# Prototype logits as extra columns of a values product, and FFN statistics and normalisation spread over the ratio attention and GpSimd

## The reference, cut to what matters

```python
x = x + _L0_xattn_ref(_layernorm(x), ctx, ctx, ...)   # distance attention
x = x + _L0_attn_ref(_layernorm(x), ...)              # ratio attention, causal
x = x + _L0_ffn_ref(_layernorm(x), ...)               # 4-bit weights, activations quantised
x = x + _L1_xattn_ref(_layernorm(x), ctx, ...)        # context attention
x = x + _L1_attn_ref(_layernorm(x), ...)              # segment attention
x = x + _L1_ffn_ref(_layernorm(x), ...)               # two of eight experts

# in _L0_ffn_ref: one scale for the whole tensor, from its largest magnitude
scale = jnp.maximum(jnp.max(jnp.abs(x)) / qmax, 1e-12)
x = jnp.clip(jnp.round(x / scale), -qmax - 1.0, qmax) * scale

# in _L1_attn_ref, x the normalised input (32 tokens a batch, 8 prototypes)
long_out = _mha(x, lt_w_in, lt_b_in, lt_w_out, lt_b_out, H)
seg = jnp.argmax(x @ protos.T, axis=-1)
same = seg[:, :, None] == seg[:, None, :]
short_out = _mha(x, st_w_in, st_b_in, st_w_out, st_b_out, H, mask=same)
short_out = jnp.where((tok_cnt == 1)[..., None], x, short_out)
combined = jnp.concatenate([long_out, short_out], axis=-1) @ fus_w.T + fus_b
```

## Time and profile before

| what | us |
|---|---|
| median of 3 runs | 754.5 (753.74 to 754.9) |
| the profiled execution | 752.91 |
| its span | 751.1 |
| TensorE busy | 662.8 (88% of the span), weight loads 500.4 |
| VectorE busy | 485.5 (65%) |
| ScalarE busy | 365.0 (49%) |
| GpSimd busy | 310.1 (41%) |
| distance attention | 0 to about 262 |
| ratio attention | about 262 to 334 |
| FFN, from its statistics to the down products | about 334 to 447 |
| context attention | about 447 to 500 |
| segment attention | about 500 to 613 |
| experts | about 613 to 751 |

### The profile page before, as it was taken

The page is one execution under the profiler, slowest core; times in us unless marked ns, Lnnn a source line. Parts: engine busy times, 40 slices in busy tenths (PEclk is TensorE's granted clock), DMA queues, the critical chain, the costliest instruction groups (busy, mean ns, idle before and its releaser), DMA issues.

```text
span 751.1 us, 16917 instructions
## 1 busy us (share of the span) xinstructions
PE 662.8 (88%) x6115; PEld 500.4 (67%) x6115; DVE 485.5 (65%) x1367; ACT 365.0 (49%) x992; POOL 310.1 (41%) x458
## 2 busy tenths in 40 slices
PE   4899999999999989985994799988999776999990
PEld 3677878787777778753443586667877673777760
DVE  2686777677768669885488873558888875333330
ACT  1454545545555479874395653436566431222320
POOL 1235455646453179850000031136556513556541
PEclk9999999999999999996997699999999986999995
DMA  8723222322220000019200434538001022243434
GB/s 265 245 62 79 64 78 65 78 65 75 68 72 14 1 3 4 3 44 332 103 0 1 156 125 177 217 125 367 2 3 65 3 99 53 47 69 58 68 40 70
DMA packets 31697, 65.08 MB, mean 87 GB/s; under 512 B 5792, under 2 KB 21792, under 8 KB 29312
## 3 DMA queue, kind: packets, MB, share of 16 engines
q1 hardware_dynamic: 26016, 55.73, 22.8%
q0 software_dynamic: 4688, 7.18, 6.0%
q10 hardware_dynamic: 912, 1.10, 0.5%
HBM read 57.67 MB, written 7.37 MB: 87 GB/s over the span
## 4 chain that ended last, share of the span: by engine, by line
PE 64%; DVE 21%; ACT 5%; issue 4%; DMA 2%; SPq 2%; POOL 1%; DVEq 0%; ACTq 0%; POOLq 0%
PE psum L2627 7%; PE psum L474 6%; PE psum L482 6%; PE psum L496 5%; PE psum L2637 4%; PE psum L521 4%; PE psum L507 4%; PE psum L1482 3%; PE psum L1459 3%; PE psum L837 2%; DVE ff_peak L1500 2%; PE psum L846 2%; PE psum L829 2%; PE psum L877 2%; DMA wn<-in_w_down 2%
## 5 line engine op out<-in xcount | busy, mean ns | idle before, releaser
L415 ACT ACTIVATE prob<-s_sb,negm 128x257 f32<-128x257 f32 x128 | 66.2, 517 | 94.5 <-DVE negm L640 94.5
L782 POOL TENSOR_SCALAR bias<-dist,cst 128x257 f32<-128x257 f32 x128 | 59.8, 486 | 99.5 <-DVE dist L627 89.6
L636 DVE CUSTOM_DVE_ANT_0 s_sb<-psum,bias 128x257 f32<-128x257 f32 x128 | 49.4, 423 | 51.7 <-PE psum L496 48.4
L474 PE MATMUL psum<-ctxT,shared 128*128 128x257 f32 x256 | 62.6, 388 | 2.7 <-DMA msk<-in_mask 2.7
L482 PE MATMUL psum<-shared,ctxT 128*128 128x256 f32 x256 | 60.4, 379 | 0.0
L2627 PE MATMUL psum<-ex_w,shared 128*128 x184 | 58.3, 460 | 0.6 <-ACT shared L2520 0.6
L1721 POOL TENSOR_TENSOR wn<-wn,cst 128x1 f32<-128x1 f32 x8 | 4.7, 589 | 120.4 <-DVE wn L1848 120.4
L474 PEld LDWEIGHTS psum<-ctxT,shared 128*128 128x128 f32 x256 | 47.2, 195 | 9.0 <-issue 3.4
L482 PEld LDWEIGHTS psum<-shared,ctxT 128*128 128x128 f32 x256 | 48.4, 189 | 6.8
L496 PE MATMUL psum<-kT,qbd 64*128 64x257 f32 x256 | 48.4, 429 | 3.0 <-DVE mx L636 2.9
L2627 PEld LDWEIGHTS psum<-ex_w,shared 128*128 128x128 f32 x184 | 33.1, 190 | 15.4 <-issue 0.8
(11 more groups left out here) (359 smaller groups left out, 1655.9 us busy)
## 6 DMA issues: line engine op xcount, KB each, us to landing
ctxT<-in_ctx_T SPq DMA_DIRECT2D x32, 257.0 KB
ex_w<-in_w SPq DMA_DIRECT2D x1, 5632.0 KB, 17.5
kpos<-in_kpos SPq DMA_DIRECT2D x32, 128.5 KB
msk<-in_mask SPq DMA_DIRECT2D x32, 128.5 KB
near_turned<-in_ctx_T_tiles SPq DMA_DIRECT2D x4, 1028.0 KB
ff_used_up<-in_ctx_T_tiles SPq DMA_DIRECT2D x4, 1028.0 KB
near_rows<-in_ctx_tiles SPq DMA_DIRECT2D x4, 1024.0 KB, 8.0
ff_used_up<-in_ctx_tiles SPq DMA_DIRECT2D x4, 1024.0 KB, 7.3
```

The costliest lines, as they stand in the source:

```text
L415: nc.scalar.activation(prob[n % 2][:, g, :], s_sb[n % 2][:, g, :], ACT.Exp, bias=negm[:, b, g:g + 1], accum_out=esum[t % 2][:, b, g:g + 1]) \
L474: ins = nc.tensor.matmul(kv[m][:, 0:SK], w["xa_k"][:, k, P * m:P * m + P], ctxT[n % BT][:, k, :], start=(k == 0), stop=(k == KT - 1))
L636: nc.vector.tensor_tensor_reduce(s_sb[n % 2][:, g, :], sc[g % 2][:, 0:SK], bias[n % 2][:, g, :], 1.0, float("-inf"), ALU.add, ALU.max, mx[ ...
L782: nc.gpsimd.tensor_scalar(bias[n % 2][:, g, :], dist[n % 2][:], c.slope[:, g:g + 1], 1.0, ALU.mult, ALU.mult).then_inc(bias_ready, 1)
```

## The change

It does the following:

- A class `FeedNorm` holds statistics, variances and roots of the FFN's input. It is allocated ahead of the ratio attention. VectorE's `feed_stats(n)` (statistics, aggregate, variance of one tile) is called in ratio slots 3 to 7 for tiles 0 to 4, between the subtraction of the maximum and the wait for the exponential; for tiles 5 and 6 right after slot 7; and for tile 7 once it is done.
- GpSimd raises the variances in three groups (tiles 0 to 4, 5 and 6, 7), and normalises the tiles of the first group itself. VectorE normalises the other three and takes three magnitudes instead of two.
- The prototypes stand as 8 more columns beside the lt input weights. The values product of an lt attention computes 264 columns, the last 8 of them logits. The logits product, the load of `protos` and their own turn in `v_use` go.
- TensorE computes the values of attention u+2 in step u, right behind its queries and keys and ahead of the scores of u+1. ScalarE copies them in the same step into one of two buffers, and with an lt attention's values the logits into SBUF. VectorE's `argmax` waits for that copy and reads SBUF.

```diff
+class FeedNorm:
+    GROUPS = ((0, 5), (5, 7), (7, 8))
+    def __init__(self, sb, sem):
+        self.stats, self.mv = sb("ff_stats", [P, NT, 6]), sb("ff_mv", [P, NT, 2])
+        self.veps, self.rstd = sb("ff_veps", [P, NT]), sb("ff_rstd", [P, NT])
+        self.veps_ready, self.rstd_ready = sem("ff_veps_ready"), sem("ff_rstd_ready")
...
+        def feed_stats(dve, n):
+            ff = after_ratio
+            dve.wait_ge(y_done, n + 1)
+            st.link(dve, nc.vector.bn_stats(ff.stats[:, n, :], x[:, n, :]))
+            st.link(dve, nc.vector.bn_aggr(ff.mv[:, n, :], ff.stats[:, n, :]))
+            ins = nc.vector.tensor_scalar(ff.veps[:, n:n + 1], ff.mv[:, n, 1:2], LN_EPS, None, ALU.add)
+            if n + 1 in [last for first, last in ff.GROUPS]:
+                ins.then_inc(ff.veps_ready, 1)
...
             if there(u + 5):
                 norm_stats(dve, u + 5)
+            for n in {3: (0,), 4: (1,), 5: (2,), 6: (3,), 7: (4,)}.get(u, ()):
+                feed_stats(dve, n)
             if there(u):
                 dve.wait_ge(p_ready, u + 1)
...
-        for i, at in enumerate((slice(0, FIRST), slice(FIRST, NT))):
-            pool.wait_ge(veps_ready, i + 1)
-            nc.gpsimd.tensor_tensor(rstd[:, at], veps[:, at], c.half[:, at], ALU.pow).then_inc(rstd_ready, 1)
+        for i, (first, last) in enumerate(feed.GROUPS):
+            pool.wait_ge(feed.veps_ready, i + 1)
+            nc.gpsimd.tensor_tensor(feed.rstd[:, first:last], feed.veps[:, first:last], c.half[:, first:last],
+                                    ALU.pow).then_inc(feed.rstd_ready, 1)
+            if i == 0:
+                pool.wait_ge(feed.rstd_ready, 1)
+                for t in range(first, last):
+                    ins = nc.gpsimd.tensor_scalar(xn[:, t, :], x[:, t, :], feed.mv[:, t, 0:1], feed.rstd[:, t:t + 1],
+                                                  ALU.subtract, ALU.mult)
+                ins.then_inc(first_normed, 1)
...
         ratio.dve(dve, NT - 1)
-        dve.wait_ge(ratio.y_done, FIRST)
-        stats_of(0, FIRST)
-        variance(0, 0, FIRST)
+        ratio.feed_stats(dve, NT - 3)
+        ratio.feed_stats(dve, NT - 2)
         ratio.dve_features(dve, NT - 1)
-        normed(0, 0, FIRST)
-        dve.wait_ge(ratio.y_done, NT)
-        stats_of(FIRST, NT)
-        variance(1, FIRST, NT)
-        magnitude(X, 0, xn[:, 0:FIRST, :])
-        normed(1, FIRST, NT)
-        st.link(dve, magnitude(X, 1, xn[:, FIRST:NT, :]))
-        top_of(X, 2)
+        normed(1)
+        dve.wait_ge(first_normed, 1)
+        magnitude(X, 0, xn[:, 0:5, :])
+        ratio.feed_stats(dve, NT - 1)
+        magnitude(X, 1, xn[:, 5:7, :])
+        normed(2)
+        st.link(dve, magnitude(X, 2, xn[:, 7:8, :]))
+        top_of(X, 3)
```

In the segment attention:

```diff
-            if there(t + 1):
-                v_use[("logits", "hot")[s], t + 1] = len(v_use) + 1
-            if there(u + 1, U):
-                v_use["v", u + 1] = len(v_use) + 1
+            if s == 1 and there(t + 1):
+                v_use["hot", t + 1] = len(v_use) + 1
+            if there(u + 2, U):
+                v_use["v", u + 2] = len(v_use) + 1
...
         def act_v(act, n):
             act.wait_ge(vb_full, v_use["v", n])
-            at_least(act, vbd_ready, n)
-            nc.scalar.copy(v[:], v_part).then_inc(vb_done, 1)
+            at_least(act, vbd_ready, n - 1)
+            ins = nc.scalar.copy(v[n % 2][:], v_part)
+            if n % 2 == 0:
+                at_least(act, hot_ready, n // 2)
+                ins = nc.scalar.copy(logits[:], logits_part)
+            ins.then_inc(vb_done, 1)
...
-            if there(u + 1, U):
-                act_v(act, u + 1)
+            if there(u + 2, U):
+                act_v(act, u + 2)
...
-            if s == 0 and there(t + 1):
-                pe.wait_ge(f_done, f_use["xT", t + 1])
-                pe.wait_ge(vb_done, v_use["logits", t + 1] - 1)
+            if there(u + 2, U):
+                n = u + 2
+                if s == 0:
+                    pe.wait_ge(f_done, f_use["xT", t + 1])
+                at_least(pe, q_ready, n)
+                project_qk(nc, qk_bank, w[kinds[s] + "_qkv"], xT[:, n // 2]).then_inc(qk_full, 1)
+                at_least(pe, vb_done, v_use["v", n] - 1)
+                wide_v = (D + NE, D)[s]
                 for k in range(KT):
-                    ins = nc.tensor.matmul(logits, xT[:, t + 1, k, :], w["protos"][:, k, :],
+                    ins = nc.tensor.matmul(v_bank[:, 0:wide_v], xT[:, n // 2, k, :],
+                                           w[kinds[s] + "_qkv"][:, k, 2 * D:2 * D + wide_v],
                                            start=(k == 0), stop=(k == KT - 1), skip_group_check=True)
                 ins.then_inc(vb_full, 1)
-            if there(u + 2, U):
-                n = u + 2
-                at_least(pe, q_ready, n)
-                project_qk(nc, qk_bank, w[kinds[s] + "_qkv"], xT[:, n // 2]).then_inc(qk_full, 1)
             if there(u + 1, U):
                 scores(pe, u + 1)
...
-            at_least(pe, vb_done, v_use["v", n] - 1)
-            project_tokens(nc, v_part, xT[:, n // 2], w[kinds[n % 2] + "_qkv"][:, :, 2 * D:3 * D]) \
-                .then_inc(vb_full, 1)
...
         def argmax(dve, t):
-            dve.wait_ge(vb_full, v_use["logits", t])
-            st.link(dve, nc.vector.tensor_reduce(lmax[:], logits, AX.X, ALU.max))
-            ins = nc.vector.tensor_scalar(first[:], logits, lmax[:], None, ALU.is_ge)
-            ins.then_inc(vb_done, 1)
-            dve.wait_ge(vb_done, v_use["logits", t])
+            dve.wait_ge(vb_done, v_use["v", 2 * t])
+            st.link(dve, nc.vector.tensor_reduce(lmax[:], logits[:], AX.X, ALU.max))
+            st.link(dve, nc.vector.tensor_scalar(first[:], logits[:], lmax[:], None, ALU.is_ge))
```

49 lines of the change are left out of this document (20 added, 29 removed).

## The result

The changed kernel takes 757.39 us (median of 9 runs, 755.38 to 759.02); the kernel before, run beside it on the same chip, 753.74 (9 runs, 750.13 to 755.26). The ratio of executions run side by side is 1.0043, with a 95% interval of 1.0030 to 1.0057: 3.2 us slower (the two medians are 3.65 apart). The forecast was +0.75 (755.2, range 752.2 to 758.0): right side, time inside the range, size a quarter of what came.

The account below looks back on a forecast made before the run. The chain was read as TensorE for 64% and VectorE for 21%. Terms of -1.85 + 0.6 + 1.3 + 0.7 = +0.75 us, set on the 754.5 median, gave 755.2, range 752.2 to 758.0.

Parts of the forecast that it names:

- (a): Ratio slots 3 to 7: VectorE's added statistics of five tiles, covered by ScalarE's exponential, cost nothing.
- (b): After ratio slot 7: statistics of tiles 5 and 6 leave the last ratio copy where it is; no cost.
- (e): Load of the prototypes: their DMA goes and their numbers travel with lt_qkv; effect nothing.
- (c): Ahead of the FFN: GpSimd raises five variances and normalises five tiles, costing nothing up to 0.72 us a tile.
- (d): FFN entry, after the last ratio copy: 2.70 us left in place of 4.55, so the FFN starts 1.85 sooner.
- (f): First step, inside the context attention: TensorE has the values product (1.13) where it had the logits (0.54); +0.6 us.
- (g): Segment attention: the argmax waits for ScalarE's copies, four tiles 0.4 late each, less 0.06 a tile; +1.3 us.
- The ring: Segment tile's loop of waits: turned one-hot copy, TensorE, ScalarE's copies, VectorE's argmax, and back; 7.93 us from copy to argmax.
- (h): Last two segment tiles: GpSimd's key products block VectorE's argmax, 0.35 us each; +0.7 us.
- The ring never closes: Rival, segment attention: ScalarE copies logits before VectorE gets to them; -2.4 us, 752.1; chance 0.27.
- The ring is longer: Rival, segment attention: 0.7 us late a tile over five tiles, both argmax steps blocked; +4.0 us, 758.5; chance 0.22.
- The clock takes the FFN's gain: Rival, FFN entry: TensorE's return to 2.4 GHz stays at about 352, losing 0.9 us; +1.7, 756.2; chance 0.11.

Follow-up runs that it names:

- statistics part: The kernel before with only the FFN-input statistics and normalisation edits of the diff: 753.52 us (12 runs), ratio 1.0008.
- segment part: The kernel before with only the segment attention edits of the diff: 758.31 us (6 runs), ratio 1.0081.
- The logits copied first: The kernel before with the segment part, ScalarE copying logits ahead of values under their own semaphore: 755.57 us (12 runs), ratio 1.0039.
- mended kernels: The changed kernel with GpSimd normalising two tiles, VectorE three, logits copied ahead of values: ratio 1.0009; with yT copied ahead of the exponential too: 0.9931.
- addition kernel: The changed kernel with GpSimd normalising by adding the negated mean and multiplying, instead of subtracting and multiplying: 757.17 us (12 runs), ratio 1.0034.
- yT came first: The kernel before with ScalarE copying yT ahead of the exponential in even steps: 750.57 us (9 runs), ratio 0.9948.

## Why the prediction was right, and where it was not

The sum was -1.85 + 0.6 + 1.3 + 0.7 = +0.75; its time and sign held. The sign held for a good reason, since the three losses were there and larger than summed: with a gain of 1.85 at the entry the terms as traced would still be above zero. That the time fell into the range was partly luck: the entry was wrong by 3.4, the last tiles by 1.2, and what was given back elsewhere (below) was not in the sum. Of the prediction's own signs of being wrong two came: GpSimd instructions over 0.75, and a full clock through 515 to 519. Term by term:

**(a), (b), (e): nothing.** Right. Slots 3 to 7 keep their distances: the turnings of the two traces lie 0.86 to 0.88 apart from slot 0 to slot 7, and the statistics of tiles 5 and 6 end at 335.80, before ScalarE has copied tile 7's own heads (337.09). The 0.87 is older than the change: it is there before the ratio attention.

**(c) was the step that failed.** It priced GpSimd's normalisation by L782, 0.486, with 0.72 as the far bound, and both were too low: 1.25. The form was a match in shape and operands and not in its operations. The step's own rule, 0.5 for every 0.1 beyond 0.72, gives 5 x (1.25 - 0.72) = 2.65; the top came 5.94 - 2.55 = 3.4 later than forecast. Most of the other 0.75 is that the five started later against the copy: the turning of slot 7 came 0.86 later than before, the last copy at the same time. So **(d)**, -1.85, became +1.5 at its place. That (d) was itself right is shown where the form is the fast one: 2.44 after the copy, against 2.55 forecast.

The Trainium skill (GPSIMD Engine Reference, 4.1 Engine selection), by which GpSimd is roughly as fast as VectorE with one input, fits the fast forms (0.46 to 0.56 beside VectorE's 0.41) and not the change's own, three times 0.41.

**(f) +0.6.** From the context attention's last row maximum (487.90 before, 489.50 after) to the first turning of the segment attention (505.34, 507.40) it is 17.44 and 17.90: +0.46. The halves alone agree: 17.25 with the statistics part, 17.90 with the segment part.

**(g) +1.3.** The ring was forecast at 7.93 from the copy of the turned one-hot to the argmax, and took 561.10 - 553.25 = 7.85; the wait 0.3 to 0.5, and was 0.37; the period 13.5 to 13.7, and was 13.62, 13.77 and 13.62. Over the three steady tiles it is 41.01 against 39.57, +1.4, where +1.3 was for four. The logits copied first take 0.26 a tile of it back, so ScalarE's copy is in the ring; TensorE's wait for the turned one-hot was not tested by itself.

**(h) +0.7 was little over a third of it.** The argmax took 2.72 and 2.50 in the last two tiles (574.72 to 577.44 and 590.14 to 592.64) where it had taken 1.52 and 1.76: +1.9. The price of a blocked step, near 0.8, was right, and that both steps would meet GpSimd in both tiles was the far end of the bound. The last two periods together grew by 29.32 - 27.47 = 1.85.
By the Trainium skill (SBUF — State Buffer, Who interferes with whom) VectorE with two SBUF inputs and GpSimd exclude each other, and a reduction on VectorE never contends. The rows agree with it: the product of two SBUF tiles waits for the end of GpSimd's instruction, the two reductions (0.16) do not. The comparison with a column waits too. The 1.4 that the prediction worked out behind that page was nearer than the term taken.

**The rivals.** "The ring never closes" is out: from the fourth argmax on VectorE waited for ScalarE's copy in three tiles of five (0.43, 0.37, 0.37), and in the other two it was GpSimd or the experts' statistics that had held it up ahead of the argmax. The dip of the clock, on which that rival rested for 1.4, was gone in the changed kernel's profile, but it was gone too with the statistics part alone and there with the segment part alone; between the kernel before and the changed one it was worth 0.8 (a period of 13.41 against 12.59). "The ring is longer" came near in time (758.5, against 757.39), but for another reason: the ring was as forecast, and GpSimd's price and the blocked steps made the rest. "The clock takes the FFN's gain" could not be judged on the change, which had no gain there. In all twelve profiles of the table the first gate product starts 7.0 to 7.3 after the end of the top, so a top that comes sooner is passed on that far; but the lower clock lasts another 7 to 10 from the start of the top, and on the mended kernels the rival is not excluded.

**What stays open.** The terms as the traces show them are +1.5 (entry), +0.46, +1.4 and +1.85: +5.2, and the ratio says +3.2 (2.3 to 4.3). The halves alone say +0.6 (-1.1 to +2.3) and +6.1 (3.8 to 8.4). And the addition in GpSimd, worth 3.5 at its place, moved the ratio by 0.0009, 0.7 us. Something gives back part of what the entry gains or loses. For the two profiles it can be read off. Their spans differ by 3.1: +0.9 before slot 7, -0.9 from there to the last copy, +1.5 at the entry, +0.5 from there to the segment attention, +2.2 in it, and -1.1 in what follows. The -0.9 goes with the clock (0.76 granted against 0.64), and +2.2 is not the whole of (g) and (h) because a dip is missing. The -1.1 behind the last turning has no cause here: the granted clock there is the same.
For the ratios the clock is the candidate. TensorE stood at 1.2 GHz from before 336 to about 352 in some profiles and from about 343 to 351 in others. And in each kernel the executions with a lower mean clock are the longer ones: of the kernel before, beside the addition kernel, the four at 0.959 took 749.5 to 750.3, the twenty at 0.944 to 0.951 took 753.2 to 756.1. The addition kernel took 752.1 to 752.7 in its three executions at 0.957 to 0.959, and the change 755.4 to 756.1 in its three at 0.957, some 3 less, which is what the entry promised; but at 0.948 they are alike (757.9, against 758.0 and 758.3). With one profile of each kernel it can't be shown that an edit there changes the odds.

## What to carry to other kernels

Price an instruction by a row with the same operations, not only the same engine, shape and operands; on GpSimd the pair of operations decided between 0.5 and 1.2. A copy on ScalarE that stands behind one with a later source is worth moving: read for each copy when its source was done, not only who waits. An instruction moved earlier can meet GpSimd where it did not before: look at what runs beside its new place. And a stage that lies next to an idle TensorE can't be judged by medians of a few runs; the distance between two instructions of the trace can, if the granted clock between them is read as well.

## What the runs showed of the hardware

- GpSimd's tensor_scalar on 128x256 float32: 0.46 to 0.56 (once 0.73) for two multiplications or a multiplication and an addition in either order, 1.15 to 1.31 (in two traces one of five 1.44 and 1.48) for a subtraction with a multiplication, two additions, or a maximum and a multiplication. On VectorE the subtraction and multiplication takes 0.41.
- VectorE's comparison of a 128x8 SBUF tile with a column, 0.23 alone, was held to 1.07 and let go within 0.03 of the end of a GpSimd instruction; a reduction of such a tile, 0.16, went through beside it. The comparison that read its tile from PSUM took 0.23 beside GpSimd's products.
- GpSimd's power of two columns took 0.70 to 0.73 in most traces, 0.84 to 0.88 in three, and 0.93 where VectorE's normalisations ran beside it.
- VectorE's product of two SBUF tiles of 128x256, 0.43 in the kernel before, took 1.00 to 1.02 beside GpSimd's products once yT came first.
- Work that no edit touches, from slot 7's turning to the last ratio copy, took 6.09 in the profile with 1.00 granted from 333 to 342, and 9.09 in the one with 0.50.
